# Experts and attention of a Trainium2 kernel: earlier row fetches, tiles cleared one by one, results read back by the next stage

## The reference

```
x = x + ssm(ctx, layernorm(x))
x = x + experts(layernorm(x))
x = x + cross_attention(layernorm(x), ctx, positions)
x = x + mlp(layernorm(x))
```

```
probs = softmax(x @ router_w.T);  top1_w, top1_idx = max, argmax of probs
w_q   = clip(round(weight / 0.5), -1, 1) * scale[:, None]
for e in range(32):
    y   = x @ (w_q * mask_e).T
    out = where(top1_idx == e, y * top1_w, out)
```

## Time and profile before

| what | value |
|---|---|
| median of 3 runs | 1829.29 us (1825.97 to 1833.02) |
| profiled execution, device time | 1830.79 us |
| its span | 1828.3 us |
| PE, DVE, ACT, POOL busy | 1490.6, 1364.8, 911.1, 683.9 us |
| granted PE clock, mean | 0.92 |
| HBM read, written | 134.11 MB, 12.85 MB |

### The profile page before, as it was taken

The page is one execution under the profiler, slowest core; times in us unless marked ns, Lnnn a source line. Parts: engine busy times, 40 slices in busy tenths (PEclk is TensorE's granted clock), DMA queues, the critical chain, the costliest instruction groups (busy, mean ns, idle before and its releaser), DMA issues. The chain is left out here.

```text
span 1828.3 us, 20886 instructions
## 1 busy us (share of the span) xinstructions
PE 1490.6 (82%) x6523; PEld 615.0 (34%) x6523; DVE 1364.8 (75%) x2030; ACT 911.1 (50%) x1201; POOL 683.9 (37%) x462
## 2 busy tenths in 40 slices
PE   5997998976742873599889988998899379999997
PEld 1333433332221421333243334324432133343433
DVE  6989999899985854589678946866793788657453
ACT  4766565663330100447654763685376254546453
POOL 3999999999924235100100010001001033333332
PEclk7899999998875997789999999999999689999998
DMA  7455455555487544300000000000000720000000
GB/s 235 127 154 147 141 146 141 153 148 142 123 196 183 122 111 156 121 1 1 1 1 1 1 1 1 1 1 1 1 1 1 157 65 1 23 1 24 1 24 23
DMA packets 65210, 131.52 MB, mean 72 GB/s; under 512 B 11328, under 2 KB 11328, under 8 KB 64336
## 3 DMA queue, kind: packets, MB, share of 16 engines
q1 hardware_dynamic: 53056, 104.07, 20.0%
q0 software_dynamic: 7168, 25.17, 6.0%
q10 hardware_dynamic: 4880, 0.95, 0.3%
HBM read 134.11 MB, written 12.85 MB: 80 GB/s over the span
## 5 line engine op out<-in xcount | busy, mean ns | idle before, releaser
L363 POOL TENSOR_TENSOR ssm_dBu<-ssm_du,ssm_BC 128x1024 f32<-128x1024 f32 x128 | 303.7, 2378 | 17.5 <-DVE ssm_du L399 17.5
L258 PE MATMUL ssm_psY<-ssm_hC,ident 128*128 128x512 f32 x512 | 254.2, 627 | 43.8 <-POOL ssm_hC L370 29.6
L1459 DVE TENSOR_REDUCE att_next_mx<-att_next_ring 128x1 f32<-128x512 f32 x384 | 241.9, 684 | 32.7 <-PE att_next_ring L1209 31.0
L327 ACT ACTIVATE ssm_dA<-ssm_delta,ssm_negA 128x512 f32<-128x512 f32 x256 | 165.4, 682 | 169.7 <-DVE ssm_hC L419 168.3
L1363 ACT ACTIVATE att_next_Pr<-att_next_psT 128x1024 f32<-128x1024 f32 x192 | 186.2, 1023 | 88.5 <-PE att_next_psT L1233 87.9
L1597 POOL TENSOR_TENSOR mlp_both<-mlp_first,mlp_third 128x512 f32<-128x512 f32 x88 | 124.7, 1417 | 256.7 <-DVE mlp_first L1799 175.4
L1799 DVE SCALAR_TENSOR_TENSOR mlp_first<-mlp_psQ,mlp_s_gu,mlp_first 128x512 f32<-128x512 f32 x176 | 131.5, 749 | 110.0 <-ACT mlp_first L1691 90.2
L1473 POOL TENSOR_TENSOR X<-X,att_bout 128x512 f32<-128x512 f32 x12 | 15.9, 1351 | 491.2 <-SPq L1120 491.2
L464 DVE TENSOR_TENSOR_SCAN ssm_dA<-ssm_dA,ssm_dBu 128x512 f32<-128x512 f32 x144 | 174.6, 1223 | 20.8 <-ACT ssm_dA L327 14.2
L1623 PE MATMUL mlp_psQ<-mlp_xh,mlp_Vgu 128*128 128x512 f16 x352 | 141.4, 402 | 50.3 <-ACT mlp_Vgu L1679 27.6
L258 PEld LDWEIGHTS ssm_psY<-ssm_hC,ident 128*128 128x128 f32 x512 | 96.8, 198 | 192.7 <-issue 100.1
(11 more groups left out here) (313 smaller groups left out, 2479.8 us busy)
## 6 DMA issues: line engine op xcount, KB each, us to landing
ssm_BC<-bc_rows SPq DMA_DIRECT2D x128, 512.0 KB, 4.8
moe_W<-in_masksT POOLq DMA_DIRECT2D x32, 512.0 KB, 7.8
mlp_words<-in_gate_upT SPq DMA_DIRECT2D x32, 176.0 KB, 7.4
X<-in_x SPq DMA_DIRECT2D x4, 1024.0 KB, 10.7
rows<-moe_XP SPq DMA_DIRECT2D x4, 1024.0 KB, 27.8
moe_XP<-results SPq DMA_DIRECT2D x4, 1024.0 KB, 9.1
out_x<-X SPq DMA_DIRECT2D x4, 1024.0 KB, 4.3
mlp_Wd<-in_downT SPq DMA_DIRECT2D x8, 352.0 KB, 15.3
```

The source lines that it names most:

```text
L258: nc.tensor.matmul(psY[:, w, :], ident[:], hC[:, w, g % RC, :], start=False, stop=(n == DS - 1)).then_inc(summed, 1)
L327: nc.scalar.activation(dA[:, q % RA, :], delta[:, b % 2, e, :], ACT.Exp, scale=negA[:, e, n:n + 1]).then_inc(dA_done, 1)
L363: nc.gpsimd.tensor_tensor(dBu[:, g % RB], du[:, b % 2, hh * W:(hh + 1) * W, :], BC[:, g % RING, 0, :].unsqueeze(1).broadcast_to([P, W, S]) ...
L1459: nc.vector.tensor_reduce(mx[:, m % 3, qt, row_order(j)], bank(("score", i)), AX.X, ALU.max).then_inc(maxed, 1)
```

## The change

1. POOL's queue in the experts: 6 masks (0 to 5) are asked for first instead of 16; behind the wait for the four stores come masks 6 to 11; then, as soon as IDX is known, the 4 fetches. XP is cleared tile by tile: 4 tiles behind the 4 fetches, then one behind each later fetch, and DVE waits in step k only for the first k + 1. Masks 12 to 20 follow one per tile.
2. POOL's queue at the end of the experts: the scatter of tile t - 1 is issued behind the scaling of tile t.
3. PE reads the next expert after the second matmul of a product, and the number of its buffer after the sixth.
4. The experts end when the scatters have landed. `results` is read by the attention: batch 0 into a new tile `back`, ahead of the context and the weights in SP's queue; batches 1 and 2 into `heads` and `xo`, which are not yet in use; batch 3 into `back` once DVE has added batch 0. DVE adds batch 0 in the preparation, the 12 other tiles two at a time behind `low_parts(2)` to `low_parts(7)` of the first batch. `gate` lives outside the stage.
5. The preparation no longer waits for the weights: PE waits for them where it first needs them, SP for the last ones in the first batch. The experts clear 35 semaphores instead of 40, the first batch 43 instead of 36.

The core of the diff (cut):

```diff
+    EARLY, SECOND = 6, 12
...
                 sp.wait_ge(returned, 16 * TILES)
-                for b in range(B):
-                    sp.dma_start(XP[:, b * NT:(b + 1) * NT, :], resT[:, b * NT:(b + 1) * NT, :]).then_inc(got[b], 16)
...
+                def clear(t):
+                    nc.gpsimd.memset(XP[:, t, :], 0.0).then_inc(zeroed, 1)
...
-                for e in range(TILES):
+                for e in range(EARLY):
                     load_mask(e)
                 for b in range(B):
                     pool.wait_ge(stored[b], 16)
-                pool.wait_ge(turned, TILES)
-                nc.gpsimd.memset(XP[:], 0.0).then_inc(zeroed, 1)
+                for e in range(EARLY, SECOND):
+                    load_mask(e)
                 pool.wait_ge(idx_done, 1)
                 for t in range(XR):
                     fetch(t)
+                for t in range(XR):
+                    clear(t)
                 for t in range(TILES):
                     if t + XR < TILES:
                         pool.wait_ge(parts, t + 1)
                         fetch(t + XR)
-                    if TILES + t < NW:
-                        load_mask(TILES + t)
+                        clear(t + XR)
+                    if SECOND + t < NW:
+                        load_mask(SECOND + t)
...
-                for t in range(TILES):
-                    pool.wait_ge(acc_done, t + E)
-                    nc.gpsimd.tensor_tensor(XP[:, t, :], XP[:, t, :], scale[:], ALU.mult).then_inc(scaled, 1)
-                    pool.wait_ge(scaled, t + 1)
-                    pool.indirect_dma_start(out=results, out_offset=bass.IndirectOffsetOnAxis(ap=IDX[:, t:t + 1], axis=0),
-                                            in_=XP[:, t, :], in_offset=None).then_inc(returned, 16)
+                for t in range(TILES + 1):
+                    if t < TILES:
+                        pool.wait_ge(acc_done, t + E)
+                        nc.gpsimd.tensor_tensor(XP[:, t, :], XP[:, t, :], scale[:], ALU.mult).then_inc(scaled, 1)
+                    if t >= 1:
+                        pool.wait_ge(scaled, t)
+                        pool.indirect_dma_start(out=results, out_offset=bass.IndirectOffsetOnAxis(ap=IDX[:, t - 1:t], axis=0),
+                                                in_=XP[:, t - 1, :], in_offset=None).then_inc(returned, 16)
...
-                    dve.wait_ge(zeroed, 1)
+                    dve.wait_ge(zeroed, min(k + 1, TILES))
...
-                        if q == DT and k + 1 < STEPS:
-                            ahead = expert(k + 1)
+                        if q == 1 and k + 1 < STEPS:
+                            next_e = expert(k + 1)
+                        if q == DT + 1 and k + 1 < STEPS:
+                            next_slot = slot_of(k + 1, next_e)
...
+                    def fetch_back(k):
+                        sp.dma_start(returned_to[k][:], resT[:, k * NT:(k + 1) * NT, :]).then_inc(back_in[k], 16)
...
-                    sp.wait_ge(loaded, 64)
-                    sp.wait_ge(ctx_in[0], 16)
+                    sp.wait_ge(added, NT)
+                    fetch_back(B - 1)
...
+                    dve.wait_ge(back_in[0], 16)
+                    for t in range(NT):
+                        nc.vector.scalar_tensor_tensor(out=X[:, t, :], in0=back[:, t, :], scalar=gate[:, t:t + 1], in1=X[:, t, :],
+                                                       op0=ALU.mult, op1=ALU.add).then_inc(added, 1)
...
+                            if first and k == 0:
+                                pe.wait_ge(ctx_in[0], 16)
+                                pe.wait_ge(wkv_in, 16)
+                            if first and k == ORDER.index((0, 0)):
+                                pe.wait_ge(wq_in, 16)
...
                             low_parts(k)
+                            if first and k >= 2:
+                                for t in (NT + 2 * (k - 2), NT + 2 * (k - 2) + 1):
+                                    dve.wait_ge(back_in[t // NT], 16)
+                                    rest.mark(nc.vector.scalar_tensor_tensor(out=X[:, t, :], in0=returned_to[t // NT][:, t % NT, :], scalar=gate[:, t:t + 1], in1=X[:, t, :],
+                                                                             op0=ALU.mult, op1=ALU.add))
```

More of the change, by code:

```diff
@@ L591, in stage_experts @@
             "cum", "ranked", "pos_done", "tables", "parts", "evac", "zeroed"))
[L592 to L593 removed]
+        W_done, mm_done, g_done, acc_done, scaled = (sem(n) for n in (
+            "W_done", "mm_done", "g_done", "acc_done", "scaled"))
         stored = [sem(f"stored{i}") for i in range(B)]
[L595 removed]
         masks = ins["masksT"]
         rowsT = rows.rearrange("(t p) d -> p t d", p=P)
[L598 removed]
         with nc.Block() as block:
@@ L835, in _ @@
                         build(k + 2)
-                for t in range(TILES):
-                    dve.wait_ge(got[t // NT], 16)
-                    nc.vector.scalar_tensor_tensor(out=X[:, t, :], in0=XP[:, t, :], scalar=gate[:, t:t + 1], in1=X[:, t, :],
-                                                   op0=ALU.mult, op1=ALU.add).then_inc(added, 1)
             @block.tensor
@@ L873, in expert, with slot_of, product @@
                 def expert(k):
-                    e = pe.value_load(EI[0:1, k:k + 1], min_val=max(0, k - TILES + 1), max_val=min(k, E - 1))
+                    return pe.value_load(EI[0:1, k:k + 1], min_val=max(0, k - TILES + 1), max_val=min(k, E - 1))
+                def slot_of(k, e):
                     if k < NW:
-                        return k - e, e
+                        return e
                     if k - TILES + 1 >= NW:
-                        return k - e, e - NW
-                    return k - e, pe.value_load(SI[0:1, k:k + 1], min_val=0, max_val=NW - 1)
-                def product(k, t, slot):
-                    ahead = None
+                        return e - NW
+                    return pe.value_load(SI[0:1, k:k + 1], min_val=0, max_val=NW - 1)
+                def product(k, e, slot):
+                    t = k - e
                     pe.wait_ge(evac, min(k + 1, TILES))
@@ L915, in _ @@
                 at = expert(0)
+                at = (at, slot_of(0, at))
                 for k in range(STEPS):
@@ L958, in stage_attention @@
         stats = sb("stats", [P, TILES, 6])
+        back = sb("back", [P, NT, D])
+        returned_to = (back, heads, xo, back)
+        back_in = [ctx.enter_context(nc.semaphore(f"att_back_in{k}")) for k in range(B)]
+        wkv_in, wq_in, wout_in = (ctx.enter_context(nc.semaphore(f"att_{k}_in")) for k in ("wkv", "wq", "wout"))
+        resT = results.rearrange("(t p) d -> p t d", p=P)
         ctx_in = [ctx.enter_context(nc.semaphore(f"att_ctx_in{k}")) for k in range(B)]
@@ L968, in stage_attention @@
             turns_f = c_.sb("turns_f", [P, 2, TILES, FQ])
-            pos_in, loaded, consts, own, mv_done, rooted, ang_done, sin_done = (c_.sem(n) for n in (
-                "pos_in", "loaded", "consts", "own", "mv_done", "rooted", "ang_done", "sin_done"))
+            pos_in, added, consts, own, mv_done, rooted, ang_done, sin_done = (c_.sem(n) for n in (
+                "pos_in", "added", "consts", "own", "mv_done", "rooted", "ang_done", "sin_done"))
             with nc.Block() as block:
@@ L1450, in _ @@
                             low_parts(k)
+                            if first and k >= 2:
[3 more added lines that the diff above has]
+                                                                             op0=ALU.mult, op1=ALU.add))
+                        if first:
+                            rest.wait()
                         for g in range(-LAG, NG + 1):
```

31 lines of the change are left out of this document (16 added, 15 removed).

## The result

| kernel | median | lowest to highest | ratio to before (95%) |
|---|---|---|---|
| before | 1828.84 us | 1825.97 to 1833.02, 4 runs | |
| changed | 1810.97 us | 1810.02 to 1811.96, 4 runs | 0.9895 (0.9883 to 0.9908) |

What follows compares the result with a forecast made beforehand. Stages stand behind barriers, so PE's and DVE's waits in four places were taken as the bound. 14.0 + 0 + 3.1 + 18.8 - 1.3 - 0.5 = 34.1 off 1830.8 gave 1796.7 us, range 1788 to 1807.

Steps and rivals of the forecast that it cites:

- The four places: Where PE and DVE wait: experts' front, experts' steps, POOL's scaling and scattering at their end, way into the attention.
- Front: Experts' start: fewer masks ahead of the stores, fetches issued once the order is known, first product earlier; gain 14.0.
- rivals 1 and 4: Front: stores no faster alone, first product 8 late, 1819, chance 0.07; DVE's work holds up fetches, 5 us lost, 1802, 0.05.
- Rival 4: Front: DVE's work holds up the fetches until the builds end, 5 us lost, 1802; chance 0.05.
- Steps, look-ups, supply: Experts' steps: nothing waits for masks or fetches, and separating PE's look-ups gains nothing; 0.
- rival 2: Experts' steps: the look-ups hide behind matmuls, 6.9 us or somewhat less gained, 1791; chance 0.10.
- rival 5: Experts' steps 0 to 8: POOL's queue serves alternating fetches and masks more slowly, slower than before, 1839; chance 0.02.
- Scatter behind the next scaling: Experts' end on POOL: saves 0.26 on 12 tiles, the last scatter keeps its wait; gain 3.1, between 0 and 4.2.
- Hand-over: Last scatter's landing to the attention's first matmul: 15.9 us instead of 34.7, gain 18.8, between 17 and 19.3.
- next late after them is nothing: Hand-over: with the weights' loads hidden behind additions and figures, nothing else would end late.
- First batch: Attention's first batch: 12 additions mostly fit into DVE's pauses; cost 1.3, between 0 and 8.1.
- rival 3: First batch: the additions don't fit, all 8.1 us lie on the path, 1803.5; chance 0.07.

Runs made afterwards that it cites:

- clear_late: Changed kernel with POOL's first four clearings held back until DVE has written its last table: 1811.9 us, ratio 0.9896.
- lookup_old: Changed kernel with both of PE's look-ups behind the fifth matmul again: 1812.16 us, ratio 0.9901.
- front_only: Kernel before with only the edits of POOL's queue ahead of and in the experts' steps: 1820.26 us, ratio 0.9939.
- no_adds: Changed kernel without the 12 additions in the first batch, only waiting for the read-backs: 1805.56 us, ratio 0.9869.
- sp_later: Changed kernel with the loads of Wout, bout, the other three contexts and batch 3's read-back moved from the preparation into the first batch: 1807.2 us, ratio 0.9889.
- dve_scale: Changed kernel with the scaling on DVE, one step behind the accumulations, leaving POOL only the scatters at the experts' end: 1805.78 us, ratio 0.9876.
- best: Changed kernel with clear_late, sp_later, dve_scale, batch 0 read back in SP's last experts instruction, and the twelve additions moved later: 1795.6 us, ratio 0.9816.
- pool_waits: Changed kernel with POOL waiting for all 16 scatters to land at the end of its part of the experts: 1813.05 us, ratio 0.9912.
- reads_behind: Changed kernel with the read-backs of batches 1 and 2 issued behind the preparation's other loads: 1812.72 us, ratio 0.9898.

## Why the forecast was wrong

The four places and their mechanisms were right; the sizes of four terms were not, most of all that of the hand-over, where two ends of queues had been left out.

- **Front**, 14.0 against 12.6. Stores alone did land fast (546.2; 548.4 forecast) and the fetches were in time, so rivals 1 and 4 fell. By itself that was worth 14.6. The issues of the fetches took 0.94 to 1.62 us instead of the 0.94 to 1.04 that I had counted on, which nothing waited for. The step that failed is the order of the clearings: I asked whether DVE waits for them in the steps (it doesn't), and not what they do to DVE while they run. It cost 2.0 us, shown by clear_late. Rival 4 had the lock-out the other way round.
- **Steps, look-ups, supply**: 0 was right (lookup_old, front_only), so rival 2 fell, and rival 5 with the 2.78 us per step. From the first product to the first accumulation it took 6.24 us instead of 5.51, with the first product's matmuls at 3.59 instead of 3.28. I had charged nothing for a slower clock in the first steps, and the traces point to the clock, though no run was made for it: it rises to 1.00 5.4 us after the start of the first product in the changed kernel and 2.8 after it in that of before. In no_adds, which is the changed kernel up to there, it happens to rise after 2.9, and there the first product takes 3.29 us, the first accumulation comes after 5.52, and the last scatter's issue ends 129.7 us after the first product's start, that of before within 0.2. So most of the -1.0 in the table is this, and not the change.
- **Scatter behind the next scaling**, 3.1 against about 0. Two errors, which cancel: the wait shrank from 0.28 to 0.17 and not to nothing, so 12 x 0.11 = 1.3; and "the last scatter keeps its wait" overlooked that the last scaling is now followed by tile 14's scatter, and its own scatter comes 1.2 us later.
- **Hand-over**, 18.8 against 9.6, most of the miss. From the landing of the last scatter: forecast 2.5 + 0.4 + 5.7 + 2.7 + 3.5 + 1.1 = 15.9, measured 6.5 + 0.4 + 6.4 + 2.8 + 3.5 + 5.5 = 25.1. The 6.5 of the barrier hold 3.6 us of POOL's DRAIN, a row that was in the trace of before, 13 us off the path, and that I didn't look for when I took its cover away. The 5.5 hold 4.3 us of SP's issues: I had written "next late after them is nothing" and counted only the bytes up to Wkv, though the block ends when SP has issued everything, 9.7 MB at 372 GB/s. sp_later gives 4.4 of it back. The landing is 0.7 slower, with the weights behind it in the same queue; whether they are the cause was not tried.
- **First batch**, 1.3 against 3.6, of which some 3.1 come with the additions (no_adds) and 0.5 with a clock that rose later. The pairs were to fall into pauses of 1.0 to 1.5 us; a pair takes 1.41, and as I read it a rotation that is pushed pushes PE's next work too. The forecast had no term for the clock, which falls to 0.50 for 3.4 us of this stretch in every profile with the additions in place. This is rival 3 with less than half of its 8.1. The semaphores were right, 0.4 for 0.5.

Together: 12.6 - 1.0 + 9.6 - 3.6 - 0.4 = 17.2, for 17.9 in the medians. The 16.9 us missing of 34.1 are 1.4 in the front, 4.1 from the first product to the last scatter, 9.2 in the hand-over and 2.3 in the first batch, less 0.1.

## What to carry to other kernels

When a change takes away the work that filled a block's end, list the end of every queue there, the idle ones too, and ask of each what now ends last: here POOL's DRAIN and SP's issues were both in the traces and both hidden until then. A queue that only issues loads holds up a barrier as long as it issues, so a load belongs into the block that needs it, or behind the barrier. And of a reordered pair of steps, write down the last round by itself: what it gains per round it can lose once.

## What the runs showed of the hardware

- POOL's DRAIN at the end of the experts ends 5.30 us behind the end of the last scatter's issue in 13 profiles, with POOL idle meanwhile, and with no arithmetic of POOL's between the scatters too (dve_scale, best). Where POOL first waited for all scatters to land it took 5.285 us from its start (pool_waits). In the attention's blocks, where POOL issues no DMA, it ends 0.06 us behind POOL's last addition, and it takes 0.03 where POOL did nothing.
- A MEMSET on POOL holds up a TENSOR_SCALAR of 47 f32 numbers on DVE to its own end (2.25 us for 0.19), and an f16 product of two SBUF tiles beside it not at all (6.90 us for six, with or without).
- With 4 to 5 MB asked for on SP's queue and not yet moved, an issue took 5.19 us instead of 0.5 (changed kernel, 5.1 MB), and 2.5 to 3.4 us (reads_behind, 4.1 to 4.3 MB); which transfer it is makes no difference.
- The granted clock rises at different moments in executions of the same code. Between 3.1 and 6.1 us after the attention's first matmul, each us later moved the first maximum by 0.5 us (dve_scale 44.03, sp_later 45.53).
